# Attention steps in pairs with a lag of six, and products of the next stage between the last steps of a part

## The chip, the cores and the metric

The kernel runs on one core of a Trainium2 chip. The metric is the time on the device in microseconds (us) from start to end of one execution; lower is better. The engines are TensorE (PE in the rows; its weight loads are PEld), VectorE (DVE), ScalarE (ACT), GpSimd (POOL) and the queue that issues DMAs (SP). A chip's TensorE runs at one of two clock levels, 1.2 or 2.4 GHz; the profile gives the granted share of the full one.

## What is computed

The input `x` is (8, 512, 32, 32) in f32. With `gn` a group normalisation over 32 groups of channels, the reference is

```python
# layer 0
t  = cbs(gn(x), cv1_w)                  # 1x1 convolution, batch norm, silu: 512 channels
ys = [t[:, :256], t[:, 256:]]
for i in range(2):                      # two bottlenecks
    z = cbs(ys[-1], m_cv1_w[i])         # 3x3 convolution, 256 channels
    q, k, v = split(conv1x1(z, m_qkv_w[i]))          # 4 heads of 64, 1024 positions
    a = softmax(einsum('bhdi,bhdj->bhij', q, k + r) * 64 ** -0.5)
    z = einsum('bhij,bhdj->bhdi', a, v)
    ys.append(ys[-1] + silu(bn(conv1x1(z, m_cv2_w[i]))))
x1 = x + cbs(concat(ys), cv2_w)
# layer 1: a 1x1 convolution with a masked, scaled and sorted weight matrix
out = x1 + conv1x1(gn(x1), w_eff)
```

Each f32 operand is split into two f16 parts, high and low, and a product is made of three f16 products (high by high, high by low, low by high).

## The kernel before

Eight images are worked one after the other; everything of an image lies in SBUF. The kernel first writes a list of steps, `steps`, with `plan(...)`; then each engine's program runs through the same list and does its share of each step, in that order. So the place of a step in the list sets its place on all five engines. Engines wait for each other with semaphores (`once`, `until_free`).

PSUM has eight banks: two (`ps_o`) take the sums of the values, six (`ps_u`) all other products. `Banks.take(work, hold, ...)` (L85) hands out one bank or, with `pair=True`, two neighbours, the one due to be free first by a running clock of guessed durations, and notes whose release its next user has to wait for. `wide` is a ring of four SBUF tiles (`WIDES`) for what ScalarE puts out in f32, `probs` a ring of six (`PROBS`) for the two f16 parts of the exponents.

`plan_image` (L478) runs, for each image, `plan_bottleneck` (L399) twice, then the rest of `cv2`, then the normalisation for layer 1 with the eight `cv1` tiles of the next image placed between its steps, then layer 1 (`l1`) and the stores. A `cv1` step holds everything of its tile: PE's products, ScalarE's two activations, VectorE's product and low part (L903, L1064), POOL's copy of the high part (L1203).

In `plan_bottleneck`:

- Four tiles of the 3x3 convolution (half `n` of the image, half `m` of the channels), each as `conv_begin` (L359, kernel rows 0 and 1, 36 products) and `conv_end` (kernel row 2, 18 products).
- Twelve pieces (`PIECES`, L367): the projections q, k and v, with nine of the 32 maxima between them. A maximum is a pair of products (L714) whose row maxima VectorE takes (L1091); eight of them give the shift of the exponents for one group, which `shift_row` (L723) turns into a row that ScalarE copies (L874).
- 32 steps: 4 groups (half of the image `n`, pair of heads) of 8 tiles. Step `s` takes its logits (8 products, L740) into a pair of banks, ScalarE takes the exponent (L882), and the high and low parts are made in one of three ways by `s % 3`: 0, ScalarE copies (L886) and VectorE subtracts from PSUM (`p_lo`, L1101); 1, ScalarE copies and POOL subtracts (L1218); 2, POOL does both (L1214, L1218). In the list each step is preceded by the values of step `s - LAG` (`av`, 24 small products, L762 to L764), with `LAG` 4, and by the next maximum while there are any. `shift_row` for the next group stands at the seventh step of a group. After the eighth `av` of a group VectorE normalises (L1106, L1107).
- The tail: the last four `av`, four `transpose` steps (L772), and `m2` for the first half of the positions (PE's products; then `m2_add`, `m2_split`, `m2_lo` on VectorE, L1121, L1126, L1131, with POOL's copy L1222). Only then comes the next `conv_begin`, or the first `cv2` tile (24 products, after the second bottleneck); it waits for `m2_lo` of both channel halves. Then `m2` for the second half and the second such tile.

All products of the convolution, the projections, `m2`, `cv1`, `cv2` and `l1` go through one line, L582.

Of the kernel before, what the change touches and what calls it, by code (L numbers as in the profile page):

```python
# [1 line left out]

# [21 lines left out]
WIDES, PROBS, LAG = 4, 6, 4  # L24
# [77 lines left out]
def build(nc, x, cv1_w, cv1_bn, cv2_w, cv2_bn, m_cv1_w, m_cv1_bn, m_qkv_w, m_rw, m_rh, m_cv2_w,  # L102
# [18 lines left out]
    with ctx:  # L121
# [237 lines left out]
        def plan_conv_begin(i, b, m, n):  # L359
            conv_use[b, m, n] = banks.take(7.8, 50.0, ("act_tile", ("m1", i, b, m, n)))  # L360
            plan("conv_begin", i, b, m, n, conv_use[b, m, n])
# [5 lines left out]
        PIECES = (("q", 0, 0), ("k", 0, 0), ("k", 0, 1), ("q", 1, 0), ("k", 1, 0), ("v", 0), ("k", 1, 1), ("v", 1), ("q", 0, 1),  # L367
                  ("v", 2), ("q", 1, 1), ("v", 3))
# [30 lines left out]
        def plan_bottleneck(i, b, ahead):  # L399
            if not conv_use:  # L400
                plan_conv_begin(i, b, 0, 0)
                plan_conv_begin(i, b, 1, 0)
            for n in range(2):
                for m in range(HT):
                    if n == 1:
                        plan_conv_begin(i, b, m, n)
# [8 lines left out]
            for p, (kind, *at) in enumerate(PIECES):  # L415
# [5 lines left out]
                if p >= 3:  # L421
                    next(maxima)
            next(maxima)
            plan_shift_row(i, b, 0)

            o_uses = {}
            for s in range(STEPS + LAG):
                if s >= LAG:
                    g, jt = divmod(s - LAG, JT)
                    if jt == 0:  # L430
                        o_uses[g] = [o_ring.take(("dve_o", (i, b, g))) for _ in range(2)]
                    banks.clock += 0.75
                    plan("av", i, b, s - LAG, o_uses[g])
                    if jt == JT - 1:
                        plan("normalise", i, b, g)
                if s < STEPS:
                    next(maxima, None)
                    w = None
                    if way(s)[1] == "pool":
                        w = wide_ring.take(("pool_lo", ("p", i, b, s)))  # L440
                    freed_by, hold = (("act_exp", (i, b, s)), 1.4) if w else (("dve_lo", ("p", i, b, s)), 4.2)
                    use = banks.take(0.9, hold, freed_by, pair=True)
                    plan("logits", i, b, s, use, w)
                    if s % JT == JT - MAX_AHEAD and s // JT + 1 < len(GROUPS_OF):
                        plan_shift_row(i, b, s // JT + 1)
                if 1 <= s <= STEPS and way(s - 1)[1] == "vector":
                    plan("p_lo", i, b, s - 1, before)
                before = use
                if s == STEPS:
                    plan_transpose(i, b, 0, 0)  # L450
                    plan_transpose(i, b, 1, 0)
                elif s == STEPS + 1:
                    plan_transpose(i, b, 0, 1)
                    halves = [plan_m2(i, b, m, 0) for m in range(HT)]
                    next(halves[0])
                elif s == STEPS + 2:
                    next(halves[1])
                    next(halves[0])
            plan_transpose(i, b, 1, 1)
            for thread in halves:  # L460
                for _ in thread:
                    pass
            if b + 1 < NB:
                plan_conv_begin(i, b + 1, 0, 0)
            else:
                plan_cv2(i, 0, 0)
            for m in range(HT):
                for _ in plan_m2(i, b, m, 1):
                    pass
            if b + 1 < NB:  # L470
                plan_conv_begin(i, b + 1, 1, 0)
# [850 lines left out]
```

## Time and profile before

| | us |
|---|---|
| median of 3 runs | 3546.49 (3544.43 to 3547.47) |
| profiled execution, its own time | 3544.41 |
| its span, first to last instruction | 3542.7 |
| PE busy | 3121.1 (88%) |
| DVE busy | 1804.9 (51%) |
| ACT busy | 1581.9 (45%) |
| POOL busy | 1146.8 (32%) |
| granted clock, mean | 0.961 |

The profile is of one execution. A matmul's end is modelled and matmuls overlap, so PE's busy time is that of intervals joined; starts tell its pace better. A row of a timeline gives start, duration, engine, line, the operation with output <- input, its shape, and in brackets the idle time before it and what ended that. The chain that ended last lies 63% on PE, 14% on DVE, 10% on ACT and 5% on POOL.

### The profile page before, as it was taken

The numbers are of one execution on the slowest core, as the hardware profiler recorded it, in microseconds if no ns is written. First come the engines' busy times: TensorE is split into PE (matmuls) and PEld (weight loads), VectorE is DVE, ScalarE is ACT, GpSimd is POOL, SyncE is SP. The second block draws the span as 40 slices with busy tenths as digits, with TensorE's granted clock in tenths as the row PEclk, the third lists the DMA queues.
The fourth block names the chain that finished last, engine by engine and source line by source line (L and its number), as shares of the span: only waits on it lengthen the run. The fifth ranks groups of instructions, "written<-read, shape, count | busy, mean of one in ns | idle before, by whom it ended". The sixth has DMA issues, their size and how long they took to land.

```text
span 3542.7 us, 61347 instructions
## 1 busy us (share of the span) xinstructions
PE 3121.1 (88%) x27308; PEld 1581.1 (45%) x27308; DVE 1804.9 (51%) x2463; ACT 1581.9 (45%) x1822; POOL 1146.8 (32%) x824
## 2 busy tenths in 40 slices
PE   4689889989899898998989898998989989899887
PEld 4435443444444444444534444444444445445443
DVE  5536464455535464363643655454643636426453
ACT  1327373164624554263731736235552547317272
POOL 1115161062512442142610615115331335116061
PEclk8889999999999999999999999999999999999998
DMA  4100000200010000100002000110001000010001
GB/s 139 66 31 22 27 8 19 75 2 27 14 60 28 1 28 25 48 28 28 3 23 75 2 27 11 40 50 1 28 22 51 28 1 28 25 51 2 1 8 42
DMA packets 35896, 105.61 MB, mean 30 GB/s; under 512 B 12976, under 2 KB 15024, under 8 KB 32944
## 3 DMA queue, kind: packets, MB, share of 16 engines
q1 hardware_dynamic: 35632, 101.69, 8.0%
q8 instruction: 215, 3.52, 0.4%
q14 instruction: 49, 0.40, 0.0%
HBM read 80.18 MB, written 21.50 MB: 29 GB/s over the span
## 4 chain that ended last, share of the span: by engine, by line
PE 63%; DVE 14%; ACT 10%; issue 6%; POOL 5%; DMA 1%; SPq 0%; POOLq 0%; ACTq 0%; DVEq 0%
PE ps_u L582 43%; PE ps_u L740 9%; DVE row_max L1091 4%; ACT wide L882 4%; PE ps_u L714 3%; ACT ps_u L882 2%; PE ps_o L762 2%; POOL probs L1218 2%; PE ps_o L763 2%; POOL wide L1198 2%; PE ps_o L764 2%; ACT probs L886 1%; DVE wide L903 1%; PE ps_u L601 1%; DVE probs L1101 1%
## 5 line engine op out<-in xcount | busy, mean ns | idle before, releaser
L1218 POOL TENSOR_TENSOR probs<-wide,probs 128x1024 f16<-128x1024 f32 x336 | 715.3, 2129 | 599.1 <-ACT probs L886 585.7
L582 PE MATMUL ps_u<-y_pad,w_c 128*128 128x512 f16 x3456 | 777.4, 387 | 57.4 <-DVE y_pad L1131 57.4
L1091 DVE TENSOR_REDUCE row_max<-ps_u 128x2 f32<-128x1024 f32 x512 | 621.0, 1221 | 166.5 <-PE ps_u L714 166.5
L903 DVE SCALAR_TENSOR_TENSOR wide<-wide 128x512 f32<-128x512 f32 x256 | 176.2, 688 | 827.4 <-ACT wide L804 827.1
L582 PEld LDWEIGHTS ps_u<-y_pad,w_c 128*128 128x128 f16 x3456 | 338.3, 98 | 489.4 <-issue 74.1
L803 ACT ACTIVATE wide<-ps_u,par_m_t 128x512 f32<-128x512 f32 x128 | 99.5, 778 | 854.5 <-PE ps_u L582 854.5
L740 PE MATMUL ps_u<-qk 64*128 64x512 f16 x3072 | 419.4, 379 | 49.3 <-ACT shift_rows L874 19.6
L762 PEld LDWEIGHTS ps_o<-v_ext,probs 128*128 128x128 f16 x4096 | 374.8, 96 | 172.8 <-issue 129.0
L762 PE MATMUL ps_o<-v_ext,probs 128*128 128x65 f16 x4096 | 433.6, 193 | 8.4 <-POOL probs L1218 7.6
L763 PE MATMUL ps_o<-v_ext,probs 128*128 128x64 f16 x4096 | 430.8, 195 | 0.0
L764 PE MATMUL ps_o<-v_ext,probs 128*128 128x65 f16 x4096 | 428.1, 191 | 0.0
L882 ACT ACTIVATE wide<-ps_u,exp_top 128x1024 f32<-128x1024 f32 x336 | 373.2, 1111 | 26.5 <-PE ps_u L740 18.2
L763 PEld LDWEIGHTS ps_o<-v_ext,probs 128*128 128x128 f16 x4096 | 380.6, 97 | 4.6
L764 PEld LDWEIGHTS ps_o<-v_ext,probs 128*128 128x128 f16 x4096 | 381.7, 99 | 0.0
L1101 DVE TENSOR_TENSOR probs<-ps_u,probs 128x1024 f16<-128x1024 f32 x176 | 214.6, 1219 | 219.8 <-ACT probs L886 217.8
L803 ACT ACTIVATE wide<-ps_u,par_cv_t 128x512 f32<-128x512 f32 x128 | 99.3, 776 | 428.3 <-PE ps_u L582 419.3
L582 PE MATMUL ps_u<-y_pad,w_cv 128*128 128x512 f16 x1152 | 287.2, 404 | 0.0
L1207 POOL TENSOR_SCALAR z<-wide 128x512 f16<-128x512 f32 x64 | 39.5, 618 | 721.5 <-DVE wide L903 721.5
L882 ACT ACTIVATE ps_u<-ps_u,exp_top 128x1024 f32<-128x1024 f32 x176 | 191.5, 1088 | 146.2 <-PE ps_u L740 146.2
L714 PE MATMUL ps_u<-qk 64*128 64x512 f16 x1024 | 200.1, 387 | 31.9 <-DVE row_max L1091 29.2
L582 PE MATMUL ps_u<-probs,w_l 128*128 128x512 f16 x768 | 188.1, 412 | 37.1 <-DVE probs L1058 37.1
L740 PEld LDWEIGHTS ps_u<-qk 64*128 64x128 f16 x3072 | 124.7, 94 | 181.8 <-ACT wide L882 48.8
(178 smaller groups left out, 3911.5 us busy)
## 6 DMA issues: line engine op xcount, KB each, us to landing
w_c<-w_c_dram SPq DMA_DIRECT2D x15, 2304.0 KB, 8.8
xn<-in_x_dram SPq DMA_DIRECT2D x32, 512.0 KB, 5.9
o_nat<-in_x_dram SPq DMA_DIRECT2D x64, 256.0 KB, 2.6
out_dram<-qk SPq DMA_DIRECT2D x32, 512.0 KB, 2.6
w_c_dram<-w_c SPq DMA_DIRECT2D x2, 2304.0 KB, 7.9
qk<-in_L_conv_m_cv_w_dram SPq DMA_DIRECT2D x2, 1152.0 KB, 7.1
probs<-in_L_conv_m_cv_w_dram SPq DMA_DIRECT2D x2, 1152.0 KB, 10.8
probs<-in_L_conv_cv_w_dram SPq DMA_DIRECT2D x2, 1024.0 KB, 12.0
```

Of the source, the lines that this page charges most:

```text
L582: ins = e.matmul(o, lhsT, rhs, start=start and k == 0, stop=stop and k == len(pairs) - 1)
L714: ins = e.matmul(ps_u[:, use.slot + q, :], q_parts[two_rows(q), 0, pair, its], k_parts[two_rows(q), 0, pair, HH[half]], start=True, stop=True)
L740: ins = e.matmul(ps_u[:, use.slot + q, :], lhsT, rhs, start=k == 0, stop=k == 3)
L762: e.matmul(o, p_part(s, 0)[:, cols], v_ext[:, jt, h, 0:HD + 1], start=False, stop=False)
L763: e.matmul(o[:, 0:HD], p_part(s, 0)[:, cols], v_ext[:, jt, h, HD + 1:2 * HD + 1], start=False, stop=False)
L764: ins = e.matmul(o, p_part(s, 1)[:, cols], v_ext[:, jt, h, 0:HD + 1], start=False, stop=last)
L803: e.activation(wide[:, w.slot, 0:HALF], ps_u[:, use.slot, :], ACT.Tanh, scale=pt[:, t, 0:1], bias=pt[:, t, 1:2])
L882: e.activation(full, both(use), ACT.Exp, scale=1.0 / (ACTIVATION_SCALE ** 2 * HD ** 0.5), bias=exp_top[:, 0:1]).then_inc(*act_exp.up(i, b, s))
L903: e.scalar_tensor_tensor(yh, th, 1.0, yh, ALU.add, ALU.mult).then_inc(*dve_u.up(*tile))
L1091: e.reduce_max(row_max[:, g % 2, :, it, half], ps_u[:, use.slot:use.slot + 2, :], axis=AX.X).then_inc(*dve_max.up(i, b, g, half, it))
L1101: e.tensor_tensor(p_part(s, 1), both(use), p_part(s, 0), ALU.subtract).then_inc(*dve_lo.up("p", i, b, s))
L1218: e.tensor_tensor(p_part(s, 1), wide[:, w.slot, :], p_part(s, 0), ALU.subtract).then_inc(*pool_lo.up("p", i, b, s))
```

## The change

- `LAG` is 6 instead of 4. The steps are planned two at a time: values of two steps, one maximum, logits of two steps, one maximum more (two at s = 0 and 2), the shift row. `p_lo` of an even step comes right behind the logits of its pair; that of an odd step behind the first maximum of the next pair.
- Nine of the twelve pieces, with eight maxima, come before the first shift row; q(0,1) right behind it, v(3) and q(1,1) in steps 1 and 2.
- The transposes for the first half of the positions come at steps 22 and 23, and `m2` for it begins at steps 25 and 27, one of its four parts in each step after.
- In the tail, the next bottleneck's `conv_begin` is planned in quarters of nine products and `cv2` in halves of twelve, placed by `turns` between the last values, transposes and `m2` of the second half. A first half of `cv2` waits for the first bottleneck's `m2` alone.
- The convolution's products go by kernel row first, then by channel half.
- A `cv1` tile is parted: PE and ScalarE at `cv1`, VectorE and POOL at `cv1_out`. Around the normalisation for layer 1 the order is now two tiles, mean, one out, one tile, variance, two outs, then for each of four norms: the norm, a tile, an out.

```diff
-WIDES, PROBS, LAG = 4, 6, 4
+WIDES, PROBS, LAG = 4, 6, 6
...
+            use = conv_use[b, m, n] = banks.take(1.9, 50.0, ("act_tile", ("m1", i, b, m, n)))
+            for quarter in range(4):
+                plan("conv_begin", i, b, m, n, use, quarter)
+                yield
...
+        FIRST = (("q", 0, 0), ("k", 0, 0), ("k", 0, 1), ("q", 1, 0), ("k", 1, 0), ("v", 0), ("k", 1, 1), ("v", 1), ("v", 2))
+        MAXIMA_AFTER = (0, 0, 1, 1, 2, 1, 2, 1, 0)
+        LATER = {-1: ("q", 0, 1), 1: ("v", 3), 2: ("q", 1, 1)}
...
+            begins = {JT * 2 + 6: lambda: plan_transpose(i, b, 0, 0), JT * 2 + 7: lambda: plan_transpose(i, b, 1, 0),
+                      JT * 3 + 1: lambda: threads.append(plan_m2(i, b, 0, 0)), JT * 3 + 3: lambda: threads.append(plan_m2(i, b, 1, 0))}
...
+            for s in range(0, STEPS, 2):
                 if s >= LAG:
+                    plan_av(s - LAG)
+                    plan_av(s - LAG + 1)
+                next(maxima, None)
+                if late:
+                    plan("p_lo", *late)
+                    late = None
+                uses = []
+                for step in (s, s + 1):
...
+                    uses.append(banks.take(0.9, hold, freed_by, pair=True))
+                    plan("logits", i, b, step, uses[-1], w)
+                for _ in range(2 if s in (0, 2) else 1):
                     next(maxima, None)
+                if s % JT == JT - MAX_AHEAD and s // JT + 1 < len(GROUPS_OF):
+                    plan_shift_row(i, b, s // JT + 1)
+                if way(s)[1] == "vector":
+                    plan("p_lo", i, b, s, uses[0])
+                if way(s + 1)[1] == "vector":
+                    late = i, b, s + 1, uses[1]
...
+            if b + 1 < NB:
+                fill = chain(*(plan_conv_begin(i, b + 1, m, 0) for m in range(HT)))
+            else:
+                fill = chain(*(plan_cv2(i, m, 0) for m in range(CT)))
+            turns = (2, 1, 1, 0) if b + 1 < NB else (1, 1, 1, 0)
...
+            plan_av(STEPS - 6)
+            plan_av(STEPS - 5)
+            for thread in threads:
+                for _ in thread:
                     pass
+            plan_av(STEPS - 4)
+            plan_transpose(i, b, 0, 1)
+            plan_av(STEPS - 3)
+            fill_in(turns[0])
+            plan_av(STEPS - 2)
+            plan_av(STEPS - 1)
+            fill_in(turns[1])
+            plan_transpose(i, b, 1, 1)
+            fill_in(turns[2])
+            last = [plan_m2(i, b, m, 1) for m in range(HT)]
+            next(last[0])
+            next(last[1])
+            next(last[0])
+            fill_in(1)
+            next(last[1])
+            next(last[0])
+            fill_in(1)
...
             plan("gn_stats", i, 1)
+            cv1_tile(2)
             plan_gn(i, 1, "gn_mean")
+            cv1_out()
+            cv1_tile()
             plan_gn(i, 1, "gn_var")
+            cv1_out(2)
             for t in range(CT):
                 plan("norm", i, 1, t, wide_ring.take(("dve_lo", ("norm", i, 1, t))))
+                cv1_tile()
+                cv1_out()
+            cv1_tile()
+            cv1_out()
```

## Rows read from the trace of the kernel before

**Rows 1.** The page: an engine's busy us, share of the span, instructions.

```profile
PE 3121.1 (88%) x27308; PEld 1581.1 (45%) x27308; DVE 1804.9 (51%) x2463; ACT 1581.9 (45%) x1822; POOL 1146.8 (32%) x824
```

**Rows 2.** Busy time by stretches: start:end, length, each engine's busy us, granted clock, DMA.

```profile
428.00:449.00 21.00, 19.09 (x119) 9.34 (x121) 19.13 (x24) 7.11 (x11) 0.00 (x0) 0.98 0.17 73
449.00:461.00 12.00, 10.41 (x111) 4.46 (x108) 9.39 (x9) 9.57 (x9) 5.28 (x3) 0.89 0.00 0
461.00:497.00 36.00, 34.32 (x564) 20.02 (x564) 26.56 (x28) 28.64 (x28) 28.11 (x16) 1.00 0.01 2
497.00:516.00 19.00, 18.38 (x328) 11.31 (x328) 5.33 (x7) 17.16 (x17) 16.65 (x11) 1.00 0.01 2
516.00:534.50 18.50, 8.77 (x132) 6.02 (x129) 10.21 (x15) 8.47 (x12) 6.03 (x5) 0.88 0.09 30
534.50:540.40 5.90, 5.89 (x14) 2.00 (x15) 0.00 (x0) 0.00 (x0) 0.00 (x0) 0.50 0.01 3
583.00:610.00 27.00, 21.71 (x102) 9.78 (x101) 14.09 (x27) 16.05 (x21) 10.86 (x9) 0.98 0.01 1
```

**Rows 3.** PE's waits: who waited for whom, us in total, times, longest.

```profile
PE ps_u L582 <- DVE y_pad L1131: 114.9, 16, 7.2
PE ps_u L582 <- DVE probs L1058: 37.1, 8, 11.2
...
PE ps_u L740 <- ACT wide L882: 14.6, 32, 1.0
```

**Rows 4.** Timeline of PE over one step, starts and durations in us.

```profile
308.94 0.19 PE L764 MATMUL ps_o<-v_ext,probs 128*128 128x65 f16 x1
309.06 0.39 PE L714 MATMUL ps_u<-qk 64*128 64x512 f16 x2
309.29 0.81 PE L740 MATMUL ps_u<-qk 64*128 64x512 f16 x6
309.94 0.38 PE L740 MATMUL ps_u<-shift_rows,shift_unit 64*128 64x512 f16 x2
310.25 0.20 PE L762 MATMUL ps_o<-v_ext,probs 128*128 128x65 f16 x1
...
310.97 0.19 PE L764 MATMUL ps_o<-v_ext,probs 128*128 128x65 f16 x1
```

**Rows 5.** Groups by line, 449 to 520: count | busy us, mean ns | idle before.

```profile
L1218 POOL TENSOR_TENSOR probs<-wide,probs 128x1024 f16<-128x1024 f32 x21 | 44.7, 2128 | 39.3 <-ACT probs L886 38.4
L1091 DVE TENSOR_REDUCE row_max<-ps_u 128x2 f32<-128x1024 f32 x23 | 28.0, 1223 | 10.9 <-PE ps_u L714 10.9
...
L882 ACT ACTIVATE wide<-ps_u,exp_top 128x1024 f32<-128x1024 f32 x21 | 23.3, 1110 | 1.7 <-PE ps_u L740 1.1
...
L886 ACT ACTIVATE probs<-wide 128x1024 f16<-128x1024 f32 x11 | 11.6, 1057 | 0.3
...
L1214 POOL TENSOR_SCALAR probs<-wide 128x1024 f16<-128x1024 f32 x10 | 10.4, 1044 | 0.0
```

**Rows 6.** Timelines of ACT and of PE behind the second group's shift row.

```profile
465.09 0.59 ACT L874 ACTIVATE shift_rows<-ps_u 128x512 f16<-128x512 f32 x1
...
465.74 0.82 PE L740 MATMUL ps_u<-qk 64*128 64x512 f16 x6 [1.22 <-ACT shift_rows L874]
```

**Rows 7.** Timeline of the tail: one transpose step and one m2 tile.

```profile
519.55 0.63 PE L772 MATMUL ps_u<-ident,o_nat 128*128 128x128 f32 x4
...
521.38 1.46 PE L582 MATMUL ps_u<-z,w_m 128*128 128x512 f16 x6 [1.20 <-DVE z L1114]
```

**Rows 8.** Timelines of POOL and of DVE before layer 1.

```profile
598.53 3.41 POOL L1198 TENSOR_SCALAR wide<-qk,gn 128x1024 f32<-128x1024 f32 x2 [0.51 <-DVE gn L1052]
603.89 0.62 POOL L1203 TENSOR_SCALAR y_pad<-wide 128x512 f16<-128x512 f32 x1 [1.95 <-DVE wide L903]
604.49 3.98 POOL L1198 TENSOR_SCALAR wide<-qk,gn 128x1024 f32<-128x1024 f32 x2
...
603.12 0.69 DVE L903 SCALAR_TENSOR_TENSOR wide<-wide 128x512 f32<-128x512 f32 x1
```

More of the change, by code:

```diff
@@ L1 @@
 from contextlib import ExitStack
+from itertools import chain
 import concourse.bass as bass
@@ L424, in plan_bottleneck @@
             plan_shift_row(i, b, 0)
-            o_uses = {}
-            for s in range(STEPS + LAG):
-                if s >= LAG:
[L429 to L436, printed above, removed]
-                    next(maxima, None)
[L438 to L458, printed above, removed]
@@ new lines, in plan_bottleneck, with fill_in @@
+            assert late is None and LAG == 6
+            if b + 1 < NB:
[3 more added lines that the diff above has]
+            turns = (2, 1, 1, 0) if b + 1 < NB else (1, 1, 1, 0)
+            def fill_in(count):
+                for _ in range(count):
+                    next(fill, None)
+            plan_av(STEPS - 6)
+            plan_av(STEPS - 5)
+            for thread in threads:
@@ L478, in plan_image @@
+            for thread in last:
+                for _ in thread:
+                    pass
+            for _ in fill:
+                pass
         def plan_image(i):
@@ L506, in build @@
             plan(*step)
+            plan("cv1_out", *step[1:])
         for i in range(B):
@@ L780, in tensor @@
                     products(ps_u[:, use.slot, :], pairs).then_inc(*u_full.up("m2", i, b, m, n))
[L781 to L782 removed]
+                elif kind == "cv2_half":
+                    i, m, n, use, half = a
                     for k in range(HT):
[L784 to L787 removed]
+                        once(dve_lo, "m2", i, half, k, n)
+                    if half == 0:
+                        until_free(use)
+                    tiles = range(half * YT // 2, (half + 1) * YT // 2)
+                    pairs = [p for k in tiles for p in three(lambda j: w_cv2[:, j, k, m * P:(m + 1) * P], lambda j: y_half(k, j, n))]
+                    ins = products(ps_u[:, use.slot, :], pairs, start=half == 0, stop=half == 1)
+                    if half:
+                        ins.then_inc(*u_full.up("cv2", i, m, n))
                 elif kind == "l1":
@@ L1199, in gpsimd @@
                                     ALU.mult, ALU.add).then_inc(*pool_norm.up(i, slot, t))
-                elif kind == "cv1":
+                elif kind == "cv1_out":
                     i, m, n, use, w = a
```

102 lines of the change are left out of this document (58 added, 44 removed).

## The prediction

> **What bounds the kernel now.** I read the page first: TensorE (PE) is busy 88% of the span [rows 1]. A share says nothing about where the rest is, so next I read the busy time by stretches of one attention part, the second of the first image (it repeats 16 times). While scores run with the maxima (461 to 497) PE has 34.3 us of work in 36.0; in the last ten steps 18.4 in 19.0; but from 516 to 534.5 only 8.8 in 18.5, and the next 5.9 us, a full stretch of work, run at a granted clock of 0.50, the lower of the two levels (1.2 instead of 2.4 GHz) [rows 2]. The waits name the hole: the first product of the next convolution, or of cv2, waits for VectorE's `m2_lo` (L1131) 16 times, 7.2 us each, 114.9 us in all [rows 3]. So three stretches count: the score steps, which are almost full of PE work, the tail behind them, which is half empty, and the passage into layer 1, with 5.3 us idle of 27 [rows 2].
>
> **The steps: what pairing removes.** One step is 24 products of the values, then a maximum and 8 products of the logits. By the starts in [rows 4]: values 0.72/23 = 31 ns apart, so 0.75 for 24; last value to first score product 0.12, which is 0.09 more than 31 ns; maximum 0.23; logits 0.22 a pair, 0.87; last logits pair to first value 0.31, which is 0.09 to 0.10 over 0.22. A change between the two kinds of product thus costs 0.09 to 0.10, two of them 0.19 a step. In pairs they come once in two steps: 0.09 saved a step, 3 us in 32 steps. The Trainium skill says in "TensorEngine Tiling (Array Packing)", Key Properties, that a change of tiling mode drains TensorE; the rows show less than a drain, since the maximum starts at 309.06 when the product before it still has 0.07 to run. Priced as a full 0.19 to 0.39 (one product's length) a change, the same edit would bring 6 to 12 us instead of 3.
>
> **What pairing adds.** Scores live in six PSUM banks, as three pairs, and ScalarE needs longer than PE for one: exponent 1.11, copy 1.06 [rows 5]. In the old order PE alternates, and a pair of banks is asked for every 1.0 us; in the new one four are asked for in 2.2 us (maximum, logits, logits, maximum), where three exist, so the third or fourth waits for the maximum just issued: 0.38 (the product) + 1.22 (VectorE, [rows 5]). PE waited for that only seldom so far, 14.6 us in 32 waits for ScalarE's exponents [rows 3].
> I walked the eight pairs s = 6 to 21 by these prices, with the bank each would get by the due times of `Banks`. Bare PE work of a pair with two maxima: 2 x 0.75 + 2 x 0.87 + 2 x 0.23 + 0.19 = 3.9. The walk gives no wait in four of eight pairs, 0.6 to 1.6 in four (the second logits behind a maximum still being read, or the second maximum behind the late `p_lo`), and one special wait: at s = 6 the shift row takes the bank of logits 7, so it stands behind exponent, copy, exponent (3.3 us) on ScalarE, with the values of two steps queued behind it on PE: 2.3 us. The old order has the same wait behind less, 1.22 us [rows 6]. Together 8 x 3.9 + 0.5 (zeros) + 0.7 (two shift rows) + 6 = 38.2 us against 36.1 now (from values 2 to values 18, about 461 to 497.1): **2.1 us lost**, bounds 1.8 us gained (the waits only as now) and 9 lost (every pair waits once more, for 1 us).
> Start of the part (428 to 461): VectorE is the bound, 19.1 busy of 21 [rows 2]. It now has 9 maxima and 9 pieces ahead of the shift row instead of 10 and 12, so the steps begin 2 to 2.5 us earlier; the three late pieces, the six logits without values and a maximum more then come in the steps, and VectorE's sum stays the same. I get the first values at 460.5, where the old order begins values 2 at 461. With lag 6 the two orders have to be compared there (the new one issues two steps' values more in the tail): **0.5 gained**, bounds 2 gained and 2.5 lost.
> SP and POOL: POOL works 2.13 twice and 1.04 once in three steps, 5.3 us [rows 5]; PE needs 5.8 or more for the same three, and six steps of lag cover POOL's last result, so POOL does not bind here.
>
> **The last ten steps and the tail.** Now 497.1 to 534.5 is 37.4 us, then 5.9 us at half clock, which cost 2.9 more than at the full one (I take 2.7, the slow stretch being somewhat shorter in an image's other part): 40.1 together [rows 2]. In the new order the transposes and m2 of the first half run within steps 22 to 31, and conv_begin quarters or cv2 halves, which depend on none of the late results, stand between the tail's pieces. PE then must do, beside such filling: values 16 x 0.75 = 12, logits 10 x 0.87 = 8.7, changes 6 x 0.19 = 1.1, zeros and shift row 0.9, 16 transposes of 128 columns 4 x 0.65 = 2.6, two m2 2 x 1.3 = 2.6 [rows 4, 7]. That is 27.9. (The m2 of the second half come after the convolution's start in both orders, or count as the same work.) Waits: 1.4 in the steps (the transposes hold a bank out of two of the three pairs, and `p_lo` 27 is late) and about 1 in the tail of the part that goes into cv2, where ScalarE and VectorE take the cv2 tile ahead of the last transpose: 29.9 with half of that. **10.2 us gained**. What hides the chain behind the last m2 (two activations, four VectorE operations of 0.69 and a POOL copy of 0.62 for each tile, [rows 8]; some 8.5 us for both by my walk) is one m2, 1.3, and four quarters of 1.95 us: 9.1. It is a close cover: without it up to 7.2 comes back. The wait goes, and what is late next is ScalarE's copy of the shift row and the exponents. Bounds 5 and 12.
> A part: 10.2 + 0.5 - 2.1 = 8.6; times 16 = **138 us gained**.
>
> **Into layer 1.** cv1's tile on PE is parted from its use (`cv1_out`), and the groups' mean now comes after two tiles instead of one, which takes off the 1.6 us in front of it. VectorE computes the variance before it takes the tiles' results, so the factors are ready some 5 us earlier; but POOL must copy two tiles before the first norm and one between every two norms. Such a copy waits for VectorE's silu, and that for VectorE's half of the norm before: [rows 8] show this circle once, POOL idle 1.95 us between norm 2 and norm 3, with silu at 603.12 and the copy at 603.89. The new order has it three times: norm 1.7, VectorE 1.23, silu 0.69, copy 0.62, 4.3 us a turn. From a first norm at 597.0 (now 598.5) that gives the last `norm` at 612.8 against 609.7 now, so PE's wait in front of layer 1, now 37.1 us in 8 [rows 3], grows: **3.1 us lost** in 7 images (the last has no cv1), 22 us. Bounds 1 gained and 5 lost (more time at the lower clock). The other moves (order of the convolution's products, cv2 in halves) leave each product as it is: nothing, since they only part one run of products.
> **Sum:** the profiled execution took 3544.4 us (span 3542.7); 3544.4 - 138 + 22 = 3428. The median of the three is 2 us higher: **3430 us**.
>
> **The rivals.** (1) The banks don't bind: waits in the steps remain as now, each part gains 1.8 in the steps, 1.5 at the start and 11 in the tail, 14.3 x 16 = 229; less 22: 3340. For it: PE's waits there are short today, and the banks that I gave to the steps can differ from the planner's. Against it: three pairs for four requests.
> (2) The fill covers half: transposes and m2 in the last steps push ScalarE (17.2 us busy of 19 there already, [rows 2], plus 4.2 for z and silu) and the tail stays late: the tail stretch gains 4.5 instead of 10.2, so 3544 - 16 x 2.9 + 22 = 3520.
> (3) Slower: the bank wait of the pair is the rule. If each of the 16 pairs of a part waits 0.7 us more than in my walk, a part loses 2.6 instead of gaining 8.6, and the time is 3546 + 41 + 22 = 3610. It decides from 0.45 us a pair on (116 us over 256 pairs). The Trainium skill warns of this in "TensorEngine Tiling (Array Packing)", PSUM Bottleneck: packing speeds the products but not what empties PSUM. The trace bears it out in part: ScalarE at 28.6 of 36 us is not full, so it would need bad order, not lack of speed.
> (4) It doesn't do what it says: the planner's ring of `wide` or a bank makes the first filling wait for the late m2 after all. Then the tail stays at 40 and only the order of the steps changes: 3546 + 16 x 1.6 + 22 = 3594, also slower.
>
> **How the numbers follow.** Forecast (3380 to 3480) 0.50; rival 1 0.18; rival 2 0.19; rival 3 0.07; rival 4 0.06. The range leaves out half of rival 1's lower side and the two slower ones: 3335 to 3530. A difference under 0.2% (7 us) can't be told from none. Faster 0.84 (the first three, less the end of rival 2), same 0.04, slower 0.12.
>
> **What would show it.** Right: the wait L582 for L1131 gone or under 1 us each; granted clock 1.0 behind the steps; the steps with maxima at 2.3 to 2.4 us each with more PE waits for `row_max` and `wide`; a wait of some 2 us at the first shift row; POOL idle twice or more between norms and layer 1 starting later. Wrong: steps at 2.0 us (rival 1), a wait of over 3 us left before the convolution (2, 4), or over 5 us a pair (3).

## The result, and the profile after

The changed kernel takes 3617.6 us (median; 3617.3 to 3620.3) against 3547.0 of the kernel before: ratio 1.0202, 95% interval 1.0184 to 1.0220. It is 71 us slower, where 3430 us was forecast, 117 faster. The profiled execution has a span of 3615.7 us and a mean granted clock of 0.953 (before 0.961). All times here are those of executions at the ordinary clock; two of the ten executions of one version (e14) ran 1.7% and 3.5% longer than its fastest, at a lower granted clock, and are left out of its figures.

PE's waits after the change (who waited for whom: us in total, times, longest us), to be laid beside [rows 3]:

```profile
PE ps_u L814 <- DVE probs L1179: 111.8, 32, 3.5
PE ps_u L655 <- DVE probs L1136: 68.3, 8, 11.2
PE ps_u L797 <- ACT wide L960: 46.7, 48, 2.3
...
PE ps_u L788 <- ACT wide L960: 30.8, 32, 1.3
PE ps_u L788 <- DVE row_max L1169: 22.4, 57, 0.9
PE ps_u L797 <- DVE shift L1175: 22.4, 16, 1.4
```

(Lines have moved: L655 is the products' L582, L814 the logits' L740, L788 the maxima's L714, L797 the shift row's L723, L836 to L838 the values', L1179 `p_lo`, L1136 VectorE's half of a norm.) The wait for `m2_lo`, 114.9 us in [rows 3], is gone, as the change wants it. A new one of about the same size stands in its place: logits wait for VectorE's `p_lo`, 111.8 us, 3.5 us each, exactly twice in each of 16 parts (logits 4 and logits 29). And the wait in front of layer 1 grew from 37.1 to 68.3.

The second part of the first image again, cut as in [rows 2] (start:end, length, busy us of PE, PEld, DVE, ACT, POOL, granted clock, DMA):

```profile
431.00:449.00 18.00, 15.28 (x95) 7.25 (x95) 16.27 (x19) 5.14 (x8) 0.00 (x0) 1.00 0.19 81
449.00:471.00 22.00, 14.62 (x134) 6.60 (x132) 13.94 (x14) 12.44 (x13) 6.62 (x4) 0.92 0.00 1
471.00:508.00 37.00, 32.20 (x517) 19.60 (x515) 25.04 (x25) 26.39 (x27) 25.58 (x16) 0.95 0.01 2
508.00:534.50 26.50, 22.58 (x350) 14.66 (x348) 16.52 (x16) 20.66 (x23) 20.41 (x13) 0.94 0.01 2
534.50:553.00 18.50, 17.15 (x212) 10.26 (x209) 6.21 (x9) 7.74 (x10) 4.38 (x3) 1.00 0.14 44
```

The tail (last row) is full: 17.2 of 18.5 us and the full clock, against 8.8 of 18.5 before. But the first steps (449 to 471) have 7.4 us without PE work, the steps with values 4.8, and the clock falls in each of the three middle stretches.

From the starts of PE's products, the median over the eight first parts of an image, in us. In the second parts the stages up to logits 31 are alike within 1.6 us, and the last one holds layer 1 too. The last row is for the whole trace behind the setup:

| stage of a part | before | after | p_lo at once (e2) | q(1,1) moved (e9) | single, lag 4 (e3) | single, lag 6 (e6) |
|---|---|---|---|---|---|---|
| k(0,1) to logits 0 | 20.4 | 18.7 | 18.7 | 20.0 | 18.7 | 18.7 |
| logits 0 to 6 | 12.4 | 21.8 | 17.5 | 17.2 | 16.1 | 16.1 |
| logits 6 to 22 | 36.0 | 39.0 | 38.5 | 39.0 | 36.0 | 35.7 |
| logits 22 to 31 | 17.8 | 25.3 | 23.2 | 22.9 | 22.3 | 28.9 |
| logits 31 to the next part's k(0,1) | 74.1 | 60.4 | 60.7 | 60.5 | 64.9 | 60.5 |
| sum | 160.6 | 165.2 | 158.5 | 159.6 | 157.9 | 159.9 |
| time at the lower clock, whole trace | 209 | 271 | 161 | 186 | 127 | 216 |

The last stage gains 13.7 us: 3.9 are work moved into an earlier stage (two transpose steps, 1.3, and two m2, 2.6), while the values of two steps more (1.5) have come into it. The stage of logits 0 to 6 loses 9.4, of which 2.6 is moved work (v(3) and q(1,1)) and 0.5 two more maxima, and it holds the values of one step less (0.75); that of logits 22 to 31 loses 7.6 with 3.9 of moved work, and it holds the values of one step less, too.

The first of the two waits, in the first part of the second image, on PE (timeline) and on VectorE:

```profile
727.38 0.82 PE L814 MATMUL ps_u<-qk 64*128 64x512 f16 x6 [3.51 <-DVE probs L1179]
```

```profile
720.80 2.36 DVE L1169 TENSOR_REDUCE row_max<-ps_u 128x2 f32<-128x1024 f32 x2 [0.72 <-PE ps_u L788]
724.31 0.75 DVE L1158 SCALAR_TENSOR_TENSOR qk<-ps_u,qkv_unit,qk 128x512 f16<-128x512 f32 x1 [1.16 <-ACT qk L942]
724.98 1.21 DVE L1169 TENSOR_REDUCE row_max<-ps_u 128x2 f32<-128x1024 f32 x1
726.11 1.21 DVE L1179 TENSOR_TENSOR probs<-ps_u,probs 128x1024 f16<-128x1024 f32 x1
```

Logits 4 need the banks of logits 3. These are released by `p_lo` 3 (726.11 to 727.32). On VectorE that stands behind the low part of q(1,1) and the next maximum; and VectorE stands idle before it, 1.16 us, for ScalarE's cast of a projection that PE began only at 722.08. So the release of a PSUM bank is queued behind the products of the very engine that waits for the bank.

The second one, some 60 us later, VectorE and POOL:

```profile
783.93 1.38 DVE L981 SCALAR_TENSOR_TENSOR wide<-wide 128x512 f32<-128x512 f32 x1 [2.21 <-ACT wide L882]
785.34 1.41 DVE L1199 TENSOR_TENSOR wide<-wide,y_pad 128x512 f32<-128x512 f32 x1
786.78 2.50 DVE L1204 TENSOR_TENSOR wide<-wide,y_pad 128x512 f32<-128x512 f32 x1
789.21 0.20 DVE L1184 RECIPROCAL recip<-ps_o 128x8 f32<-128x8 f32 x1
789.44 0.69 DVE L1185 TENSOR_TENSOR o_nat<-ps_o,recip 128x512 f32<-128x512 f32 x1
790.05 1.21 DVE L1179 TENSOR_TENSOR probs<-ps_u,probs 128x1024 f16<-128x1024 f32 x1
791.18 1.94 DVE L1209 TENSOR_TENSOR y_pad<-wide,y_pad 128x512 f16<-128x512 f32 x1
```

```profile
784.99 1.23 POOL L1292 TENSOR_SCALAR probs<-wide 128x1024 f16<-128x1024 f32 x1 [0.23 <-ACT wide L960]
786.30 2.44 POOL L1296 TENSOR_TENSOR probs<-wide,probs 128x1024 f16<-128x1024 f32 x1
...
790.45 2.12 POOL L1296 TENSOR_TENSOR probs<-wide,probs 128x1024 f16<-128x1024 f32 x1 [0.45 <-ACT probs L964]
```

Logits 29 wait for `p_lo` 27 (790.05). Ahead of it stand silu, `m2_add`, `m2_split` and the normalising, and behind it `m2_lo`. These four m2 operations (silu is L981) take 0.69 us each in the kernel before; here they take 1.38, 1.41, 2.50 and 1.94.

Both waits, and the shift row's, are followed by a stretch at the lower clock (windows as above):

```profile
728.70:731.90 3.20, 3.20 (x34) 1.87 (x31) 1.23 (x1) 2.93 (x3) 1.16 (x1) 0.50 0.00 0
738.90:742.10 3.20, 3.20 (x28) 1.56 (x26) 1.23 (x1) 0.10 (x1) 1.63 (x1) 0.50 0.00 0
790.10:796.70 6.60, 5.38 (x60) 3.51 (x62) 5.86 (x6) 1.38 (x2) 4.29 (x3) 0.50 0.01 2
```

Before, PE had been idle 3.51, 2.26 and 3.48 us. At the lower clock the values run 55 ns apart instead of 31 (1.27 us from the first start to the last of 24, instead of 0.72). Added up over the trace behind the setup, the time at the lower clock is 271 us after and 209 before. Work that is bound by PE gets about half as far in such a stretch, so by my estimate these 62 us more are worth up to 31 of the 71 us.

### The profile page after: what moved, and what is told of

It is laid out like the page before. It is cut to its first block, busy times and chain, and to the rows that moved or that the text cites. A ratio compares the mean times of both kernels' runs of the same rounds, so it can differ in the third digit from the quotient of the medians.

```text
span 3615.7 us, 61363 instructions
## 1 busy us (share of the span) xinstructions
PE 3112.1 (86%) x27308; PEld 1618.2 (45%) x27308; DVE 1889.6 (52%) x2463; ACT 1569.1 (43%) x1822; POOL 1158.7 (32%) x824
## 4 chain that ended last, share of the span: by engine, by line
PE 63%; DVE 17%; ACT 8%; issue 7%; POOL 4%; SPq 0%; DMA 0%; POOLq 0%; ACTq 0%; DVEq 0%
PE ps_u L655 40%; PE ps_u L814 7%; DVE row_max L1169 6%; ACT wide L960 3%; PE ps_o L836 3%; PE ps_o L837 3%; PE ps_o L838 3%; PE ps_u L788 3%; DVE probs L1179 3%; ACT ps_u L960 2%; DVE qk L1158 2%; POOL wide L1276 1%; PE ps_u L674 1%; DVE wide L981 1%; DVE wide L1204 1%
## 5 line engine op out<-in xcount | busy, mean ns | idle before, releaser
L1296 POOL TENSOR_TENSOR probs<-wide,probs 128x1024 f16<-128x1024 f32 x336 | 725.0, 2158 | 736.3 <-ACT probs L964 723.0
L655 PE MATMUL ps_u<-y_pad,w_c 128*128 128x512 f16 x3456 | 769.0, 383 | 0.0
L1169 DVE TENSOR_REDUCE row_max<-ps_u 128x2 f32<-128x1024 f32 x512 | 621.3, 1222 | 275.6 <-PE ps_u L788 275.6
L814 PE MATMUL ps_u<-qk 64*128 64x512 f16 x3072 | 444.2, 397 | 132.8 <-DVE probs L1179 111.8
L981 DVE SCALAR_TENSOR_TENSOR wide<-wide 128x512 f32<-128x512 f32 x256 | 187.1, 731 | 693.7 <-ACT wide L882 693.4
L655 PEld LDWEIGHTS ps_u<-y_pad,w_c 128*128 128x128 f16 x3456 | 335.0, 97 | 418.3
L836 PE MATMUL ps_o<-v_ext,probs 128*128 128x65 f16 x4096 | 438.1, 199 | 0.0
L838 PE MATMUL ps_o<-v_ext,probs 128*128 128x65 f16 x4096 | 436.3, 198 | 0.0
L836 PEld LDWEIGHTS ps_o<-v_ext,probs 128*128 128x128 f16 x4096 | 396.7, 100 | 38.8 <-issue 25.8
L837 PEld LDWEIGHTS ps_o<-v_ext,probs 128*128 128x128 f16 x4096 | 398.5, 101 | 8.1
L838 PEld LDWEIGHTS ps_o<-v_ext,probs 128*128 128x128 f16 x4096 | 398.7, 103 | 0.0
L814 PEld LDWEIGHTS ps_u<-qk 64*128 64x128 f16 x3072 | 141.5, 97 | 316.4 <-DVE probs L1179 124.4
L788 PE MATMUL ps_u<-qk 64*128 64x512 f16 x1024 | 204.4, 394 | 87.3 <-ACT wide L960 30.8
L655 PE MATMUL ps_u<-y_pad,w_cv 128*128 128x512 f16 x1152 | 277.4, 391 | 0.0
L1179 DVE TENSOR_TENSOR probs<-ps_u,probs 128x1024 f16<-128x1024 f32 x176 | 214.3, 1217 | 112.0 <-ACT probs L964 112.0
L655 PE MATMUL ps_u<-probs,w_l 128*128 128x512 f16 x768 | 185.4, 407 | 68.3 <-DVE probs L1136 68.3
```

The costliest lines, as they stand in the source:

```text
L655: ins = e.matmul(o, lhsT, rhs, start=start and k == 0, stop=stop and k == len(pairs) - 1)
L788: ins = e.matmul(ps_u[:, use.slot + q, :], q_parts[two_rows(q), 0, pair, its], k_parts[two_rows(q), 0, pair, HH[half]], start=True, stop=True)
L814: ins = e.matmul(ps_u[:, use.slot + q, :], lhsT, rhs, start=k == 0, stop=k == 3)
L836: e.matmul(o, p_part(s, 0)[:, cols], v_ext[:, jt, h, 0:HD + 1], start=False, stop=False)
L837: e.matmul(o[:, 0:HD], p_part(s, 0)[:, cols], v_ext[:, jt, h, HD + 1:2 * HD + 1], start=False, stop=False)
L838: ins = e.matmul(o, p_part(s, 1)[:, cols], v_ext[:, jt, h, 0:HD + 1], start=False, stop=last)
```

## The experiments

Theory A: the pairs lose by the order on VectorE, by the late `p_lo` with other work ahead of it. Theory B: pairing itself loses, because four pairs of banks are asked for where three are. Theory C: the new order around the steps is what loses.

**e1, the old order at cv1**

```diff
             plan("gn_stats", i, 1)
-            cv1_tile(2)
+            whole(cv1)
             plan_gn(i, 1, "gn_mean")
-            cv1_out()
-            cv1_tile()
+            whole(cv1)
+            whole(cv1)
...
```

> The changed kernel with one part undone: cv1 tiles and the normalisation in front of layer 1 in the old order (whole tiles: one, mean, two, variance, norm, norm, tile, norm, norm, tile). Theory A (the new order makes the circle of POOL's norm, VectorE's half, VectorE's silu and POOL's copy turn three times, 2.6 us lost in each of 7 images by the two traces): 3618 - 18 = 3600 us. Rival (the passage only gives back what the changed timing before it took): no change, 3618.

3593.8 us, 24 less than the changed kernel (7 times 3.4). The passage costs what its circle says. In the changed kernel's trace, POOL in front of layer 1:

```profile
601.66 1.73 POOL L1276 TENSOR_SCALAR wide<-qk,gn 128x1024 f32<-128x1024 f32 x1
605.33 0.63 POOL L1281 TENSOR_SCALAR y_pad<-wide 128x512 f16<-128x512 f32 x1 [1.95 <-DVE wide L981]
605.94 1.73 POOL L1276 TENSOR_SCALAR wide<-qk,gn 128x1024 f32<-128x1024 f32 x1
609.62 0.62 POOL L1281 TENSOR_SCALAR y_plain<-wide 128x512 f16<-128x512 f32 x1 [1.95 <-DVE wide L981]
610.22 1.73 POOL L1276 TENSOR_SCALAR wide<-qk,gn 128x1024 f32<-128x1024 f32 x1
...
614.50 1.73 POOL L1276 TENSOR_SCALAR wide<-qk,gn 128x1024 f32<-128x1024 f32 x1
```

Norms start 4.28 us apart, with POOL idle 1.95 in each turn, where [rows 8] show two norms back to back.

**e2, p_lo of an odd step at once**

```diff
                 if way(s + 1)[1] == "vector":
-                    late = i, b, s + 1, uses[1]
+                    plan("p_lo", i, b, s + 1, uses[1])
```

> The changed kernel, but the low part (p_lo) of an odd vector step is planned right behind the logits of its pair and no longer behind the first maximum of the next pair. Theory A (the two waits of 3.5 us a part, logits 4 behind p_lo 3 and logits 29 behind p_lo 27, come from that place in VectorE's order, and each also brings 1.7 to 3.4 us at half clock): they shrink to under 1 us, 16 x 10 us less, 3618 - 160 = 3460 us. Rival B (pairs ask for four pairs of banks where three are, and any order on VectorE leaves some request waiting): the waits move to the maxima, 3590 to 3618 us.

3536.6 us, ratio to the kernel before 0.9974 (0.9964 to 0.9984): 81 us less than the changed kernel by one line, half of what theory A expected. The waits of logits for `p_lo` fall from 111.8 to 14.1 us, but others grow:

```profile
PE ps_u L814 <- DVE row_max L1169: 38.9, 32, 1.8
...
PE ps_o L829 <- DVE o_nat L1185: 29.8, 16, 1.9
...
PE ps_u L814 <- DVE probs L1179: 14.1, 32, 0.5
```

Both theories have a part. The place of `p_lo` is worth 5.1 us a part. Of the 97.7 us of waits taken away, 24.1 come back as logits that wait for maxima (14.8 before this edit), as B said, and 29.8 as the zeros product that waits for the normalising. The time at the lower clock falls by 110 us, so much of the gain is clock.

**e3, steps one at a time with lag 4, all else as changed** (the loop over single steps of the kernel before, with the new `LATER` and `begins`)

> The changed kernel with the steps one at a time and lag 4 as before (one extra maximum at s = 0), everything around the steps as changed. Theory A and B both: the steps run as in the kernel before and the tail's hole of 7.2 us is filled; 10 us less than before in each of 16 parts, some 2 to 3 of them lost again because m2's VectorE work then stands among the steps, and 18 us more in front of layer 1: 3546 - 16 x 7.5 + 18 = 3445 us. Rival C (the order around the steps is what costs, by m2 and the transposes within steps 22 to 31): 3546 or more.

3486.6 us, ratio 0.9833 (0.9819 to 0.9848). So theory C falls: the order around the steps alone gains 59 us, and 131 lie between it and the changed kernel. (It undoes pairs and lag together; e6, e7 and e11 tell them apart.) It gains less than expected, 42 us less: logits 22 to 31 take 22.3 us, where the 3.9 of moved work would make 21.7 out of 17.8; the values wait for POOL (24.7 us in 16) and the first fill for `m2_lo` (19.2 us in 8).

**e4, the kernel before with pairs and lag 6 alone**

> The kernel before with the pairs and lag 6 alone; pieces, transposes, m2, tail and layer 1 as before. Theory B (pairing itself costs, about 6 to 9 us a part): 3546 + 16 x 7.5 = 3666 us. Rival C (pairs are harmless or help, by 3 us of changes a part; the order around costs): 3500 to 3546 us.

3609.0 us, ratio 1.0178 (1.0163 to 1.0194): in the old surroundings pairs and lag lose 63 us. Its waits (L597 is the product's line here, L738 the shift row's, L729 the maxima's, L755 the logits'):

```profile
PE ps_u L597 <- DVE y_pad L1146: 115.0, 16, 7.2
PE ps_u L738 <- ACT wide L897: 46.6, 48, 2.3
PE ps_u L729 <- ACT wide L897: 41.2, 48, 1.9
PE ps_u L755 <- DVE row_max L1106: 38.8, 61, 1.1
```

The hole of the tail is as before, and 46.6 + 41.2 + 38.8 us of waits for banks are there; the shift row and the maxima have no such waits for ScalarE before, and the logits' wait for maxima was 11.1. There is no wait for `p_lo` of 3.5 us: the late place of `p_lo` is there, but q(1,1) and m2 don't stand among the steps. So the new surroundings alone gain 59 us (e3), pairs and lag alone lose 63, and together they lose 71: some 67 us come from the two meeting.

**e5, e3 and e1 together**

> Single steps with lag 4 (as e3) and cv1 around the normalisation in the old order (as e1): the two gains added. Theory A (the parts are independent, image by image): 3487 - 24 = 3463 us. If the passage and the steps hang together: 3487 or between.

3463.5 us, ratio 0.9769 (0.9755 to 0.9784), the sum to the microsecond. This is the fastest version of this study, 82 us better than the kernel before and 154 than the changed one. Its time at the lower clock is 75 us, against 209 before: 134 us less, worth up to 67 of the 82 by the same estimate.

**e6, single steps with lag 6** (`LAG` 6 in e3, two steps' values more in the tail)

> As e3, single steps, but lag 6 instead of 4. Theory A (it is VectorE's order and the place of the late p_lo, not the lag, that costs): within 10 us of e3, 3477 to 3497 us, as two steps' values only move from ahead of the steps' end to the tail, where they hide the chain. Rival D (the lag costs: six logits without values between them at the start, where VectorE and the banks bind, 1.5 us a part, and values missing as cover): 3487 + 16 x 1.5 = 3511 us.

3545.4 us: the lag alone costs 59 us, more than twice the 24 that even rival D gave it, and not where D had it. Logits 0 to 6 take 16.1 us as with lag 4, logits 22 to 31 take 28.9 instead of 22.3:

```profile
PE ps_o L819 <- DVE o_nat L1175: 70.0, 16, 4.4
```

The zeros product that begins the last group of values waits for the normalising of the group before. With lag 4 this comes at step 27, when VectorE has one silu and one `m2_add` to do ahead of it (2.8 us); with lag 6 it comes at step 29, when the whole chain of one m2 tile, a `p_lo` and half the chain of the other tile stand ahead (11 us). Logits wait for `p_lo` again, 24.6 us in 16.

**e7, e2 with the shift row ahead of its pair's logits**

```diff
                 next(maxima, None)
+                if s % JT == JT - MAX_AHEAD and s // JT + 1 < len(GROUPS_OF):
+                    plan_shift_row(i, b, s // JT + 1)
                 if late:
...
-                if s % JT == JT - MAX_AHEAD and s // JT + 1 < len(GROUPS_OF):
-                    plan_shift_row(i, b, s // JT + 1)
```

> As e2 (pairs, p_lo at once), and the shift row stands ahead of the logits of its pair instead of behind them. Theory B (it waits for the exponents of its own pair on ScalarE, 46.7 us in 48 waits, with the values of two steps behind it): these waits go, 3537 - 45 = 3490 us, near e3. Rival (PE then waits as long for a bank in another place): 3525 to 3540.

3515.1 us, 21 less than e2, not quite half of the 46.7 us that the wait had; it is gone, and the logits' wait for the maxima grew from 38.9 to 56.7 us. A wait taken away in a pair comes back in part in the next request for a bank.

**e8, the changed kernel with m2 two pairs later**

```diff
-                      JT * 3 + 1: lambda: threads.append(plan_m2(i, b, 0, 0)), JT * 3 + 3: lambda: threads.append(plan_m2(i, b, 1, 0))}
+                      JT * 3 + 5: lambda: threads.append(plan_m2(i, b, 0, 0)), JT * 3 + 7: lambda: threads.append(plan_m2(i, b, 1, 0))}
```

> The changed kernel with m2 of the first half begun at steps 29 and 31 instead of 25 and 27; everything else as changed, the late p_lo too. Theory A (logits 29 wait 3.5 us for p_lo 27, because m2_add and m2_split stand ahead of it on VectorE, each at two to three times its length while POOL works): that wait goes and its time at half clock with it, 16 x 5 = 80 us less, of which up to 2 us a part come back in the tail: 3618 - 60 = 3558 us. Rival (any order holds that bank as long): 3610 to 3620.

3624.5 us, 7 more. The cause is confirmed and the price was wrong:

```profile
PE ps_u L655 <- DVE y_pad L1209: 74.6, 16, 6.8
...
PE ps_u L814 <- DVE probs L1179: 56.1, 16, 3.5
```

The wait of logits 29 is gone (56.1 us in 16 are those of logits 4), and the hole in front of the convolution and of cv2 is back with 74.6 us. In a first part, logits 22 to 31 take 18.6 us instead of 25.3, and the stage behind them takes 70.0 instead of 60.4. The cover of the tail is as close as was said in the prediction.

**e9, q(1,1) ahead of the steps**

```diff
-        LATER = {-1: ("q", 0, 1), 1: ("v", 3), 2: ("q", 1, 1)}
+        LATER = {-1: ("q", 0, 1), 1: ("v", 3)}
...
             piece(*LATER[-1])
+            piece("q", 1, 1)
```

> The changed kernel with one move: the piece q(1,1) stands before the steps, right behind q(0,1), and not at step 2. Theory A (logits 4 wait for p_lo 3, which stands on VectorE behind the low part of q(1,1) and a maximum, and VectorE idles for q(1,1)'s products and cast): the wait of 3.5 us falls by the 2 to 3 us of that piece's way, its half clock goes too, while the steps begin 1.3 us later: 3618 - 16 x 2 = 3586 us. Rival (the late place behind a maximum alone holds it): 3610 to 3620.

3546.8 us, 71 less than the changed kernel, more than twice what was expected, by moving one projection. Its waits for `p_lo` are 55.7 us in 16, those of logits 29 alone: the one of logits 4 is gone altogether. The stage of logits 0 to 6 takes 17.2 instead of 21.8 us, the one before it 1.3 more. More comes from logits 22 to 31, although logits 29 wait as long as before, and the clock accounts for it: over both versions and all parts this stage takes 22.9 us where none of it runs at the lower clock, 24.4 where 3.4 us do, and 25.2 to 25.4 where 6.8 us do. The changed kernel has only the longer two kinds (9 and 7 parts of 16); here 9 of 16 parts are of the shortest. Over the trace the time at the lower clock is 186 us instead of 271. Why the clock falls less often behind the same wait is not shown.

**e10, e5 with transposes and m2 two steps earlier**

```diff
-            begins = {JT * 2 + 6: lambda: plan_transpose(i, b, 0, 0), JT * 2 + 7: lambda: plan_transpose(i, b, 1, 0),
-                      JT * 3 + 1: lambda: threads.append(plan_m2(i, b, 0, 0)), JT * 3 + 3: lambda: threads.append(plan_m2(i, b, 1, 0))}
+            begins = {JT * 2 + 4: lambda: plan_transpose(i, b, 0, 0), JT * 2 + 5: lambda: plan_transpose(i, b, 1, 0),
+                      JT * 2 + 7: lambda: threads.append(plan_m2(i, b, 0, 0)), JT * 3 + 1: lambda: threads.append(plan_m2(i, b, 1, 0))}
```

> As e5 (single steps, lag 4, old order at cv1), with the transposes at steps 20 and 21 and m2 at steps 23 and 25, two earlier each, which lag 4 allows. Theory A (m2's VectorE operations, drawn out by POOL, are what makes the values wait for normalise and the fill for m2_lo): those waits, 24 and 19 us in all, go: 3463 - 30 = 3433 us. Rival (they only meet the maxima of steps 20 and 21 and p_lo 24 instead): 3455 to 3470.

3523.4 us, 60 more than e5: wrong in sign. The waits for the normalising rose from 24.2 to 100.9 us, 6.0 us the longest. VectorE in front of one of them, where the zeros product starts at 771.07:

```profile
765.41 1.51 DVE L1191 TENSOR_TENSOR y_pad<-wide,y_pad 128x512 f16<-128x512 f32 x1 [2.71 <-POOL y_pad L1282]
766.84 2.60 DVE L963 SCALAR_TENSOR_TENSOR wide<-wide 128x512 f32<-128x512 f32 x1
769.48 0.69 DVE L1181 TENSOR_TENSOR wide<-wide,y_pad 128x512 f32<-128x512 f32 x1
770.09 0.20 DVE L1166 RECIPROCAL recip<-ps_o 128x8 f32<-128x8 f32 x1
770.32 0.69 DVE L1167 TENSOR_TENSOR o_nat<-ps_o,recip 128x512 f32<-128x512 f32 x1
```

`m2_lo` waits 2.71 us for its copy on POOL, which is busy with the exponents, the next silu takes 2.60 us instead of 0.69, and the normalising waits behind both.

**e11, e7 with lag 4**

> As e7 (pairs, p_lo at once, shift row early), with lag 4 instead of 6. Theory E (lag 6 meets normalise and m2 on VectorE at the group change, as in the single steps, where lag 4 was 59 us faster): 3515 - 45 = 3470 us, and the pair's own gain of 0.09 a step is then visible against e3's 3487. Rival F (in pairs the values come before POOL is done with lag 4, since step s + 3 of its pair leaves POOL only two steps): PE waits for POOL's L1296, 3515 to 3560.

3598.1 us, 83 more than with lag 6. Rival F: the values wait for POOL, 76.2 us in 64, up to 3.0 (in the changed kernel there is no such wait), and the logits for the maxima 70.1 us. So in these surroundings pairs need the lag of six, and single steps lose by it (e6).

**e12, POOL's subtraction cut to 8 columns, else as changed**

```diff
-    e.tensor_tensor(p_part(s, 1), wide[:, w.slot, :], p_part(s, 0), ALU.subtract)
+    e.tensor_tensor(p_part(s, 1)[:, 0:8], wide[:, w.slot, 0:8], p_part(s, 0)[:, 0:8], ALU.subtract)
```

> The changed kernel with POOL's subtraction (L1296, 2.16 us, 336 times) cut to 8 of 1024 columns: the low parts of two steps in three are left out, which changes the output, and nothing waits long for POOL. (The buffer is filled with zeros once, in the setup, some 10 us.) Theory G (VectorE's m2 operations among the steps, 1.4 to 2.5 us instead of 0.69, are drawn out by POOL working at the same time, and this is half of the wait of logits 29): they fall to 0.7, that wait from 3.5 to under 1.5 us, logits 4's wait of 3.5 stays, 3618 + 10 - 16 x 4 = 3564 us. Rival (they are long for another reason, ScalarE's or the banks'): they stay long, wait and time stay, 3620 to 3630.

This version leaves out the low parts of two steps in three, so it is no faster kernel but a probe. 3552.9 us, 65 less (with the filling of zeros in it, which makes the setup some 13 us longer). The groups of `m2_add`'s and `m2_split`'s additions and of `m2_lo` in the changed kernel, and then in this one (count | busy us, mean ns | idle before):

```profile
L1204 DVE TENSOR_TENSOR wide<-wide,y_pad 128x512 f32<-128x512 f32 x64 | 85.6, 1338 | 1.1
L1209 DVE TENSOR_TENSOR y_pad<-wide,y_pad 128x512 f16<-128x512 f32 x64 | 64.3, 1005 | 23.8 <-POOL y_pad L1300 23.8
L1199 DVE TENSOR_TENSOR wide<-wide,y_pad 128x512 f32<-128x512 f32 x64 | 55.7, 871 | 2.2
```

```profile
L1204 DVE TENSOR_TENSOR wide<-wide,y_pad 128x512 f32<-128x512 f32 x64 | 55.6, 868 | 1.1
L1199 DVE TENSOR_TENSOR wide<-wide,y_pad 128x512 f32<-128x512 f32 x64 | 44.3, 692 | 2.2
L1209 DVE TENSOR_TENSOR y_pad<-wide,y_pad 128x512 f16<-128x512 f32 x64 | 44.1, 690 | 23.7 <-POOL y_pad L1301 23.7
```

Without POOL's long operation beside them they are back at 0.69 us, but for those beside POOL's copy of 1024 columns. The waits of logits for `p_lo` fall to 75.1 us: 56 of logits 4, so 1.2 instead of 3.5 us each for logits 29.

**e13, e5 with m2 two steps later** (steps 27 and 29)

> As e5 (3463 us: single steps, lag 4, old order at cv1), with m2 begun at steps 27 and 29 instead of 25 and 27. Theory A (m2 ahead of normalise on VectorE holds the zeros product, 24 us in all, and is drawn out by POOL): that wait goes, but the chain ends later, with only the fill of the tail to cover it, and L1191's 19 us grow: 3450 to 3475 us. Rival (cover is ample): 3440 us.

3472.1 us, 9 more than e5. The wait for the normalising fell from 24.2 to 4.2 us, that for `m2_lo` grew from 19.2 to 58.2 us. With e10 this brackets the place: 60 us lost two steps earlier, 9 two steps later.

**e14, pairs with all of it mended** (e7, with the moves of e9 and e1)

> Pairs and lag 6 with all that was found: p_lo at once, shift row ahead of the logits, q(1,1) before the steps, old order at cv1 (e7 with the moves of e1 and e9). Theory A (q(1,1)'s move and p_lo at once mend the same wait, so the second adds little): 3515 - 24 - 5 = 3486 us, still above the single steps' 3463. Theory H (pairing is worth its 0.09 us a step once orders are right): 3463 - 45 = 3420 us.

3547.3 us, the same as the kernel before (0.9994 to 1.0014), and 61 over what theory A gave; H falls too. The single moves don't add up. Its largest waits of the steps, and then a stretch of the first steps in the first part of the second image (windows as above):

```profile
PE ps_u L809 <- DVE row_max L1164: 84.2, 64, 1.8
PE ps_u L783 <- ACT wide L955: 40.2, 48, 1.3
```

```profile
711.80:718.50 6.70, 5.64 (x63) 3.43 (x60) 2.81 (x4) 3.28 (x3) 4.05 (x4) 0.50 0.00 0
```

The first steps take 20.3 us (logits 0 to 6) against 17.9 in e7, although q(1,1), 1.3 us, is no longer among them. Two things make up for the 3.7 us. Logits wait for maxima that VectorE still reads: 84.2 against 56.7 us over the trace, 1.7 us a part. And 6.8 us of this stage run at the lower clock, where in most parts of e7 none of it does, in the part shown without any idle time of PE over 1.4 us just before. Over the trace it is 206 us at the lower clock against 130. That q(1,1) at step 2 had given VectorE time for its maxima is how I read it; no run shows it by itself.

## Why the prediction was wrong, step by step

The forecast gave 8.6 us gained a part; measured are 4.6 lost in the first part of an image and 2.3 in the second, once the 3.3 that e1 shows for layer 1 are taken out. That is 11 to 13 us a part, some 190 us in 16 parts.

- **What pairing removes**: right. In full clock the changes cost 0.08 to 0.10 each in the changed kernel too (last value to maximum 0.12 to 0.13 where no wait lies between), once in two steps.
- **The steps with values, s = 6 to 21**: mechanism right and size nearly. Forecast 38.2 us from the first values to values 16 (its own terms add up to 38.4); measured 39.8 in the first parts and 39.1 in the second, 3.4 us of them at the lower clock, which the forecast did not have. The special wait of the shift row, forecast at 2.3, is 2.26 us. It is the only stretch that the prediction walks pair by pair.
- **The start of the part**: this step failed, by 6 us a part, about 100 us in all. It said "VectorE's sum stays the same. I get the first values at 460.5", 32.4 us behind k(0,1); measured 38.1 and 38.5. (The old order's values 2, with which it compares, come 31.7 us behind k(0,1) in 15 of 16 parts; the part that I read is the exception, with 32.8. So the loss against the kernel before is 6.4 and 6.8 us.) I summed VectorE's work as if it never stood idle and only its sum counted. But the late `p_lo` 3 was put behind q(1,1), whose products PE had yet to do, and PE's next logits stood behind `p_lo` 3. e2 and e9 each take this away (4.3 us of logits 0 to 6, and 4.6, of which 1.3 are q(1,1)'s own products, done earlier).
- **The last ten steps and the tail**: the gain forecast is 10.2, measured 5.4 and, without layer 1's loss, 7.4. The fill works as forecast: no wait in the tail but 1.35 us ahead of m2 in the part before cv2, forecast as about 1. What failed is the term "Waits: 1.4 in the steps", in which "`p_lo` 27 is late" was one wait among others: logits 29 alone wait 3.5 us for it, and up to 6.8 us at half clock follow. VectorE's m2 operations were priced at 0.69 us, their time without POOL beside them; e12 shows 2.3 of the 3.5 us to be POOL's (1.2 are left without its long subtraction), e8 shows that m2's place ahead of `p_lo` causes it.
- **The clock**: a term that was missing. I took it as given back by the filled tail, and each wait of 2.3 to 3.5 us in the steps took it again: 3.2, 3.2 and 6.6 us at the lower level in the first part of the second image (rows above). Over the trace it is 62 us more, not less. What the runs leave open is when exactly a wait brings it: e9 has the same wait of logits 29 in every part and the lower clock behind it in only some.
- **Into layer 1**: right, in mechanism (three turns of 4.28, forecast 4.3) and size: 24 us by e1, forecast 22.
- **SP and POOL**: "POOL does not bind here" holds for the values' waits, which are nil, but POOL bound VectorE, which I had not looked at.
- **The rivals**: rival 3 gave 3610 us and came nearest to the time. Its mechanism, a wait in every pair, is not what happened: two waits a part of 3.5 us in two places, and the place was the start and the end of the steps, not the pairs between; that its time is near is luck. The pressure on banks that it named does show in e4, where pairs and lag alone lose 63 us, and in e2, e7 and e14, each of which moves a wait to the maxima. Rivals 2 and 4 did not occur: the filled tail works.

What stays open is why moves that help alone don't add in e14. Its traces show what is lost, 1.7 us a part of waits for maxima and 76 us more at the lower clock than e7, but not why the banks come in that order. I read it as the planner handing out banks by due times that don't hold in pairs; no run of this study changes those times, so that is argued, not shown.

## What to carry to other kernels

An operation that releases a scarce buffer must stand in its engine's queue ahead of everything that the waiting engine has yet to produce; walk every engine's order at the start and the end of a loop, not only its steady part and its sum of work. When work is moved to fill an idle stretch, price each engine's share beside its new neighbours: here the move was worth 59 us with single steps, and pairing and the longer lag took 131 away. A lag or a grouping is not good or bad by itself: lag 6 cost single steps 59 us and lag 4 cost pairs 83. And beside the waits, add up the time at the lower clock in every version: here it went from 75 to 295 us, and it explains differences that the list of waits does not.

## What the runs showed of the hardware

VectorE and POOL get in each other's way when both read SBUF, and it is no even sharing. An operation of VectorE on two SBUF operands (0.69 us alone) ended 0.55 us behind the end of the POOL operation that ran when it began, three times in the rows above: 785.34 + 1.41 against 786.22, 786.78 + 2.50 against 788.74, 791.18 + 1.94 against 792.57. It is no matter of chance: all 79 operations of L1199, L1204, L1209 and L981 in the changed kernel's trace that began while POOL worked ended 0.53 to 0.55 us behind POOL's. So it looks as if each waited for POOL's operation and then ran for most of its own length. It goes the other way too: the 31 subtractions of POOL that began while one of these ran took 2.44 us, those with none beside them 2.13. VectorE's reads from PSUM beside POOL (L1179, L1169, 1.21 us) are not longer. The Trainium skill has this in "SBUF — State Buffer", Who interferes with whom: an instruction of VectorE with two SBUF inputs contends with a GpSimd instruction that reads SBUF, and whichever starts second is held until the first is done. By that rule the trace agrees, with 0.55 us left after POOL's end.

PE's granted clock fell to the lower level after idle times of 3.51, 2.26 and 3.48 us inside the steps, and the rows above show it there for 3.2, 3.2 and 6.6 us, in the first two with PE busy all the time. In e14 it fell for 6.8 us (711.75 to 718.58) behind idle times of 1.35, 1.13, 0.80 and 0.74 us only.
